# A three-block network on one core: part of VectorE's elementwise work moved to GpSimd, a residual factor folded into a weight, and new instruction orders

## The chip, the cores and the metric

The kernel runs on one core of a Trainium2 chip. The time is the device time of one execution in microseconds, for the whole program: loading of the weights, their preparation, and 16 samples. The kernel before was run three times: 1011.65, 1012.00 and 1012.29 us, median 1012.0.

## The reference, cut to what matters

Input `x` has 16 samples of 256 tokens and 128 channels. Each goes through two blocks with layer norms around them; the first is a state-space mixer with an MLP, then attention with an MLP, the second a gated feed-forward network of width 512. The lines that matter here:

```python
h = layernorm(x)                                  # x0 of the first block
xm = resid_mix_m[0] * h + resid_mix_m[1] * h      # first mix
Bm, Cm = xm @ B_proj_w, xm @ C_proj_w             # 16 heads of 64
value, gate = split(rms_norm(xm) @ in_proj_w)     # 256 + 256
value = silu(causal_conv(value))
y = selective_scan(value, A, Bm, Cm, dt) + D_param * value
y = (y * silu(gate)) @ out_proj_w                 # gate product
xm = xm + mamba_scale * y
xm = xm + m_mlp_scale * (relu(rms_norm(xm) @ m_fc_w) ** 2 @ m_proj_w)
xa = resid_mix_a[0] * xm + resid_mix_a[1] * h     # second mix
...                                               # attention, o_proj, MLP: xa
x1 = x + layernorm(xa)
f = silu(n @ w1) * (n @ w2)                       # n = layernorm(x1)
f = gelu(gelu(f @ h1) @ h2) @ w3
out = x1 + layernorm(f)                           # last addition
```

## The kernel before, in words

A sample of 256 tokens is two tiles of 128 tokens. Elementwise work on tokens has the shape 128x256 (two tiles of 128 channels); the transposed work has channels on the partitions and 256 tokens along the row. Products that need more precision are split in a high and a low part: ScalarE writes the rounded high part, VectorE or GpSimd subtract it for the low part, and TensorE makes three products (hi x hi, lo x hi, hi x lo). That is `xmT_hi`/`xmT_lo` after xm_turn, `nT`, `n2T`, `xT`, and `hD_hi`/`hD_lo` of the feed-forward block, whose low part GpSimd makes in four subtractions a sample (two in hd_part at L612 ahead of hidden1, two in hc_part at L617 ahead of hidden2).

All 16 samples run through nine chains of steps, named by letters: N (load, norm), M (projections, convolution), S (the scan), D (output projection, MLP, second mix), H (head of attention), K (row maxima), A (weights and values), T (tail of attention, its MLP), F (feed-forward). W is the preparation of the weights, run once. A step is a small function on each engine that takes part in it. Every engine has an order written out by hand, a string of letters in `TURNS`: for each letter the engine takes the next step of that chain, whichever sample it is at. So an engine works on up to seven samples at a time, and in the regular part of the program it goes from the scan of sample i to the feed-forward block of sample i-6. An engine never overtakes its own order; between engines there are semaphores. `BANKS` says, in the same way, which of the eight PSUM banks each step of TensorE takes; its former holder must have been read out. `FILL` says before which TensorE steps how many filling products, of the identity with itself and of no use to the result, are made.

Names that matter here: `xh` the normalised input, `xm` the mixer's stream, `val`/`yg` one buffer for value and gated value, `gate` the gate, `xa` the stream of the attention block, `rows` the channel factors (R_M0, R_A0, R_A1), `LM` the decay matrices of the scan, `P` the exponentials (P01, P2), `sl` the evacuated attention output, `bank` any PSUM bank. The steps on the way of the change:

- norm_in, norm_in2 (VectorE, GpSimd, ScalarE): statistics, layer norm into `xh` (L953), first mix into `xm` (L978), squares and norm of `xm`.
- mask (VectorE, L1011): scan products times `LM`; va (TensorE) multiplies by the values; yg (VectorE, L1016 and L1019) adds D and multiplies by the gate; m_out (TensorE) projects.
- m_norm (VectorE, L1032): `xh` times R_A1. m_res (VectorE, L1039, L1041, L1043): adds the MLP's sum, multiplies by R_A0, adds `xh` into `xa`.
- wts (TensorE, QT,KT), wt (ScalarE, L827, exponential), pmask (GpSimd, L549), pv (TensorE, P,Va), y_rows (TensorE, from `sl`).
- f_norm (VectorE, L953 and L1216): last layer norm and last addition.
- GpSimd also makes every reciprocal root, as a pair of tiny instructions (L501, L503), the two squares in each MLP (L527, L560) and, at the start, the preparation of weights (L581 to L607).

Of the kernel before, what the change touches and what calls it, by code (L numbers as in the profile page):

```python
# [48 lines left out]
    ssq_f=TILES, rs_f_eps=1, rs_f=1, nrm_f=1, n2_hi=1, hid_f=2, mlp_f=1, mlp_free=1, mix=2, xa=1,  # L49
# [38 lines left out]
def _chains():  # L88
# [4 lines left out]
    front = [("load_x", 0), ("norm_in", 0), ("norm_in2", 0), ("nrm_in", 0)]  # L93
    mixer = [("xm_turn", 0), ("n_turn", 0)] + several("gates", 2) + several("conv", 2) + [("val", 0), ("val_turn", 0)]
    mixed = several("m_out", 2) + [("m_add", 0), ("m_sq", 0), ("m_norm", 0), ("n2_turn", 0)]
# [3 lines left out]
    for u in range(KINDS):  # L99
# [112 lines left out]
def program(nc, t, out):  # L212
# [167 lines left out]
    def wait_free(engine, c, i, n):  # L380
# [101 lines left out]
    def _(pool):  # L482
# [100 lines left out]
        def by_row(w, r, nk):  # L583
            g.tensor_tensor(w[:], w[:], r.unsqueeze(1).to_broadcast([P, nk, D]), ALU.mult)
# [1042 lines left out]
```

## Time and profile before

| | |
|---|---|
| runs | 1011.65, 1012.00, 1012.29 us |
| profiled execution | 1011.6 us, of which the span from first to last instruction is 1009.9 |
| granted TensorE clock, mean | 0.994 |
| TensorE busy | 934.5 us, 93% |
| VectorE busy | 707.6 us, 70% |
| ScalarE busy | 649.3 us, 64% |
| GpSimd busy | 388.1 us, 38% |
| bytes moved | 14.49 MB, mean 14 GB/s |

The busy share of TensorE counts its filling products as well. The first 250 us bring the samples one after another into the pipeline, the last 180 us drain it. The rows on which the prediction rests have a section of their own below.

### The profile page before, as it was taken

What the parts mean: (1) busy time and instruction counts of PE and PEld (TensorE: products, weight loads), DVE (VectorE), ACT (ScalarE), POOL (GpSimd) and SP (SyncE); (2) the same over time, 40 slices, a digit from 0 to 9 for tenths busy, and PEclk for the clock granted to TensorE, in tenths of its full rate; (3) what the DMA queues carried; (4) which work ended last, traced back from release to release, by engine and by line L of the source; (5) the groups of instructions that cost most, each with busy time, mean ns of one, the idle gap of its engine ahead of it and who ended that gap; (6) DMA issues with size and microseconds to landing.
All of it is one profiled execution on the core that took longest, in us unless ns stands there. A gap on an engine that the chain in (4) does not pass through costs nothing.

```text
span 1009.9 us, 25012 instructions
## 1 busy us (share of the span) xinstructions
PE 934.5 (93%) x9570; PEld 805.3 (80%) x9570; DVE 707.6 (70%) x2075; ACT 649.3 (64%) x1513; POOL 388.1 (38%) x625
## 2 busy tenths in 40 slices
PE   6889999998999989999999999899999999999996
PEld 6778788766978878697878878697878877878896
DVE  4556898977878676968868686968868686853330
ACT  3654546858658577775757677775757678578541
POOL 2553112325143333525244343525244336355421
PEclk9999999999999999999999999999999999999999
DMA  7000000000000000000000000000000000000000
GB/s 272 1 1 7 7 6 2 13 2 12 2 17 2 1 18 1 18 1 17 2 17 2 6 14 1 18 2 17 2 17 2 7 6 7 12 7 7 16 6 6
DMA packets 17206, 14.49 MB, mean 14 GB/s; under 512 B 1857, under 2 KB 15553, under 8 KB 16833
## 3 DMA queue, kind: packets, MB, share of 16 engines
q1 hardware_dynamic: 17088, 12.89, 4.0%
q8 instruction: 78, 1.28, 0.5%
q14 instruction: 40, 0.32, 0.1%
HBM read 10.79 MB, written 2.10 MB: 13 GB/s over the span
## 4 chain that ended last, share of the span: by engine, by line
PE 61%; ACT 17%; DVE 8%; POOL 7%; issue 5%; DMA 0%; SPq 0%; POOLq 0%; ACTq 0%; DVEq 0%
PE bank L1233 57%; POOL hD_lo L617 4%; ACT P L827 3%; POOL hD_lo L612 2%; ACT h L860 2%; PE bank L1244 2%; ACT junk L668 2%; ACT L860 1%; DVE cv L998 1%; DVE mneg L1140 1%; DVE M L1011 1%; ACT sl L835 1%; ACT BC L675 1%; ACT LM L662 1%; POOL P L549 1%
## 5 line engine op out<-in xcount | busy, mean ns | idle before, releaser
L549 POOL TENSOR_SCALAR_AFFINE_SELECT P<-P 128x256 f32<-128x256 f32 (+1 forms) x192 | 94.2, 506 | 181.2 <-ACT P L827 175.9
L1011 DVE TENSOR_TENSOR M<-bank,LM 128x384 f32<-128x384 f32 x256 | 126.7, 550 | 50.7 <-PE bank L1233 50.5
L1233 PE MATMUL bank<-hD_hi,w_h_hi 128*128 128x256 f32 x512 | 147.7, 289 | 12.6 <-POOL hD_lo L617 9.5
L1233 PE MATMUL bank<-hD_hi,w_h_lo 128*128 128x256 f32 x512 | 143.4, 280 | 0.0
L1233 PE MATMUL bank<-hD_lo,w_h_hi 128*128 128x256 f32 x512 | 143.4, 280 | 0.0
L1140 DVE TENSOR_REDUCE mneg<-bank 128x2 f32<-128x512 f32 (+1 forms) x192 | 121.6, 682 | 12.1 <-PE bank L1233 12.0
L827 ACT ACTIVATE P<-bank 128x512 f32<-128x512 f32 x192 | 101.2, 612 | 17.6 <-PE bank L1233 16.8
L1233 PEld LDWEIGHTS bank<-hD_hi,w_h_hi 128*128 128x128 f32 x512 | 96.4, 188 | 17.7 <-POOL hD_lo L617 12.8
L866 ACT ACTIVATE h<-bank,cols 128x256 f32<-128x256 f32 x128 | 53.2, 471 | 87.6 <-PE bank L1233 87.1
L675 ACT ACTIVATE BC<-bank 128x512 f32<-128x512 f32 x128 | 75.1, 606 | 51.2 <-PE bank L1233 48.8
L1233 PE MATMUL bank<-BC 64*128 64x256 f32 (+1 forms) x1024 | 101.0, 336 | 4.7 <-ACT BC L675 2.9
L1233 PEld LDWEIGHTS bank<-BC 64*128 64x128 f32 x1024 | 84.2, 187 | 20.1 <-ACT BC L675 5.6
L1233 PEld LDWEIGHTS bank<-hD_lo,w_h_hi 128*128 128x128 f32 x512 | 96.5, 188 | 0.0
L1233 PEld LDWEIGHTS bank<-hD_hi,w_h_lo 128*128 128x128 f32 x512 | 96.3, 188 | 0.0
L617 POOL TENSOR_TENSOR hD_lo<-h,hD_hi 128x512 fp32r<-128x512 f32 x32 | 42.7, 1355 | 105.6 <-ACT hD_hi L876 105.6
L1233 PE MATMUL bank<-ident 128*128 128x128 f32 x514 | 71.7, 285 | 12.1 <-DMA M<-in_w_in 7.5
L1233 PEld LDWEIGHTS bank<-ident 128*128 128x128 f32 x514 | 64.8, 198 | 16.0 <-issue 8.6
L942 DVE BATCH_NORM_STATS2 ostat<-bank 128x6 f32<-128x128 f32 x32 | 7.9, 290 | 89.9 <-PE bank L1233 89.9
L998 DVE SCALAR_TENSOR_TENSOR cv<-vpad,cols,cv 128x256 f32<-128x256 f32 x96 | 53.2, 555 | 3.4
L1233 PE MATMUL bank<-M,xpad 128*32 128x256 f32 (+1 forms) x1024 | 54.1, 332 | 1.0 <-DVE M L1011 0.9
L527 POOL TENSOR_TENSOR hid<-hid 128x512 f32<-128x512 f32 x32 | 33.4, 1050 | 53.4 <-ACT hid L773 53.1
L612 POOL TENSOR_TENSOR hD_lo<-h,hD_hi 128x512 fp32r<-128x512 f32 x32 | 40.7, 1283 | 32.1 <-ACT hD_hi L715 31.5
(252 smaller groups left out, 2599.0 us busy)
## 6 DMA issues: line engine op xcount, KB each, us to landing
xh<-in_x SPq DMA_DIRECT2D x16, 128.0 KB, 2.1
P<-in_w_h SPq DMA_DIRECT2D x2, 1024.0 KB, 8.2
x_res<-in_x SPq DMA_DIRECT2D x16, 128.0 KB, 2.3
out<-out_sb SPq DMA_DIRECT2D x16, 128.0 KB, 2.2
M<-in_w_B SPq DMA_DIRECT2D x1, 512.0 KB, 4.3
M<-in_w_C SPq DMA_DIRECT2D x1, 512.0 KB, 4.8
Qs<-in_w SPq DMA_DIRECT2D x2, 256.0 KB, 4.3
M<-in_w_in SPq DMA_DIRECT2D x1, 256.0 KB, 3.2
```

Source lines behind the costliest of these rows:

```text
L527: g.tensor_tensor(two, two, two, ALU.mult).then_inc(S["hid_f"], 1)
L549: g.affine_select(p3, p3, [[0, parts], [1, P]], ALU.is_ge, zero, base=0, channel_multiplier=-1).then_inc(S["pmask"], 1)
L612: g.tensor_tensor(hD_lo[:, two, :], h[:, two, :], hD_hi[:, two, :].bitcast(F32), ALU.subtract).then_inc(S["hd_lo"], 1)
L617: g.tensor_tensor(hD_lo[:, two, :], h[:, two, :], hD_hi[:, two, :].bitcast(F32), ALU.subtract).then_inc(S["hc_lo"], 1)
L675: a.activation(dst, psum(c, i, n) if src is None else src, ACT.Copy).then_inc(evac(c, n), 1)
L827: a.activation(PT[c][:, j, :], psum("A", i, n), ACT.Exp).then_inc(evac("A", n), 1)
L860: a.activation(h[:, j, :], psum_t("F", i, F_W + j), ACT.Silu, scale=cols[:, C_W1 + j:C_W1 + j + 1]).then_inc(S["silu"], 1)
L866: last = a.activation(h[:, j, :], psum("F", i, n)[:, k * TOK:(k + 1) * TOK], ACT.Gelu, scale=cols[:, c + j:c + j + 1])
L998: v.scalar_tensor_tensor(cv[:, b, :], vpad[:, b, j:j + L], w(j), cv[:, b, :], ALU.mult, ALU.add).then_inc(S["conv"], 1)
L1011: last = v.tensor_tensor(M[:, k % 2, r, e, :], psum("C", i, 2 * n + e)[:, 0:TRI], LM[:, h + e, :, :].rearrange("p a q -> p (a q)"), ALU.mult)
L1140: v.reduce_max(neg, of, axis=AX.X, negate=True).then_inc(evac("K", n), 1)
L1233: return p.matmul(o, lhsT, rhs, start=start, stop=True, skip_group_check=True)
```

## The change

Five edits go together.

1. The residual factor R_A0 = resid_mix_a[0] is multiplied into the weight `w_mpj` of the mixer's MLP, once at the start, on GpSimd. The sum that `down` leaves in PSUM then already has the factor.
2. The second mix gets a step m_mix on GpSimd, of three instructions: `xh` times R_A1, `xm` times R_A0, and their sum into `xh`. On VectorE m_norm's product is gone, and of m_res one addition is left, `xh` plus PSUM into `xa`.
3. The gate product (yg) goes from VectorE to GpSimd. VectorE keeps the addition of D ahead of it.
4. The first mix (mix_in) and, with it, the sum of the two factors at sample 0, goes to GpSimd.
5. The last addition (f_norm) goes to GpSimd; VectorE keeps the layer norm ahead of it.

`TURNS`, `BANKS` and `FILL` are new for all engines. There are 257 filling products before and 241 after. The diff, cut to its core:

```diff
-    ssq_f=TILES, rs_f_eps=1, rs_f=1, nrm_f=1, n2_hi=1, hid_f=2, mlp_f=1, mlp_free=1, mix=2, xa=1,
+    ssq_f=TILES, rs_f_eps=1, rs_f=1, nrm_f=1, n2_hi=1, hid_f=2, mlp_f=1, by_a1=1, by_a0=1, mix=1, xa=1,
...
-    front = [("load_x", 0), ("norm_in", 0), ("norm_in2", 0), ("nrm_in", 0)]
+    front = [("load_x", 0), ("norm_in", 0), ("mix_in", 0), ("norm_in2", 0), ("nrm_in", 0)]
...
-    PE=("MMMMMMSSSSSMSMMSSSSSSSDSSSSDSSSSMSSSSSSSSDSDDSSDDDDHDHMDDMDDSMSMSSSSMSSHSSSSHSDSMSKSKMSSSSMDKMSDDDMSSDSDSSSKSSHSDMSSMKSM"
+    PE=("MMMMMMSSSSSSMMSSSSSSSSDSSSSMDSSSMSSSSSSSSDSDDSSDDDDHHDDDMMDSSMMSSSDSMSSHSSSSSMHSKMKSSSSSMDDSSMKDDMDSSDSDSSSSSKSMHSSMKSMS"
...
# GpSimd
+        def mix_in(i, _):
+            if i == 0:
+                pool.wait_ge(first_in, 16 * len(first_w))
+                g.tensor_tensor(rows[:, R_M0, :], rows[:, R_M0, :], nrm[:, 0, :], ALU.add).then_inc(row_in, 1)
+                pool.wait_ge(row_in, 1)
+            if i > 1:
+                pool.wait_ge(S["xa"], i - 1)
+            pool.wait_ge(S["nrm_n"], 2 * i + 1)
+            g.tensor_tensor(xm[i % 2][:], xh[i % XBUF][:], by_channel(R_M0), ALU.mult).then_inc(S["xm"], 1)
+
+        def yg_(i, b):
+            pool.wait_ge(S["yacc_free"], at(i, "yacc_free", b + 1))
+            g.tensor_tensor(yg[:, b, :], yg[:, b, :], gate[:, b, :], ALU.mult).then_inc(S["yg"], 1)
+
+        def m_mix(i, _):
+            x, r = xh[i % XBUF], xm[i % 2]
+            pool.wait_ge(S["xm"], i + 1)
+            g.tensor_tensor(x[:], x[:], by_channel(R_A1), ALU.mult).then_inc(S["by_a1"], 1)
+            pool.wait_ge(S["nrm_f"], i + 1)
+            g.tensor_tensor(r[:], r[:], by_channel(R_A0), ALU.mult).then_inc(S["by_a0"], 1)
+            pool.wait_ge(S["by_a0"], i + 1)
+            g.tensor_tensor(x[:], x[:], r[:], ALU.add).then_inc(S["mix"], 1)
+
+        def f_norm(i, _):
+            pool.wait_ge(S["nrm_o"], i + 1)
+            g.tensor_tensor(out_sb[:], out_sb[:], x1[i % 2][:], ALU.add).then_inc(S["out_ready"], 1)
...
         def w_mix(i, _):
             pool.wait_ge(mixer_in, 16 * len(mixer_w))
             by_row(w_out, rows_m[:, R_MS, :], 2)
-            by_row(w_mpj, rows_m[:, R_MM, :], NBLK)
+            by_row(w_mpj, rows_m[:, R_MM, :], NBLK).then_inc(mpj_scaled, 1)
+            pool.wait_ge(mpj_scaled, 1)
             pool.wait_ge(mix_half, 1)
+            by_row(w_mpj, rows[:, R_A0, :], NBLK)
...
# VectorE
         def norm_in2(i, _):
             x = xh[i % XBUF]
-            if i > 1:
-                dve.wait_ge(S["xa"], i - 1)
             dve.wait_ge(S["rs_n"], 2 * i + 1)
             layer_norm(x, x, nmv, nrs).then_inc(S["nrm_n"], 1)
...
-            dve.wait_ge(S["nrm_n"], 2 * i + 1)
-            v.tensor_tensor(xm[i % 2][:], x[:], by_channel(R_M0), ALU.mult).then_inc(S["xm"], 1)
...
-            dve.wait_ge(S["yacc_free"], at(i, "yacc_free", b + 1))
-            v.tensor_tensor(yg[:, b, :], yg[:, b, :], gate[:, b, :], ALU.mult).then_inc(S["yg"], 1)
...
-        def m_norm(i, _):
-            x = xh[i % XBUF]
-            dve.wait_ge(S["xm"], i + 1)
-            v.tensor_tensor(x[:], x[:], by_channel(R_A1), ALU.mult).then_inc(S["mix"], 1)
...
         def m_res(i, _):
...
+            dve.wait_ge(S["mix"], i + 1)
             dve.wait_ge(S["mlp_f"], i + 1)
-            v.tensor_tensor(flat(x), flat(x), psum_t("Y", i, 1), ALU.add).then_inc(S["mlp_free"], 1)
-            dve.wait_ge(S["mlp_free"], i + 1)
-            v.tensor_tensor(x[:], x[:], by_channel(R_A0), ALU.mult).then_inc(S["mix"], 1)
-            dve.wait_ge(S["mix"], 2 * i + 2)
-            v.tensor_tensor(xa[i % ABUF][:], x[:], xh[i % XBUF][:], ALU.add).then_inc(S["xa"], 1)
+            v.tensor_tensor(flat(xa[i % ABUF]), flat(xh[i % XBUF]), psum_t("Y", i, 1), ALU.add).then_inc(S["xa"], 1)
...
         def f_norm(i, _):
...
-            dve.wait_ge(S["nrm_o"], i + 1)
-            v.tensor_tensor(out_sb[:], out_sb[:], x1[i % 2][:], ALU.add).then_inc(S["out_ready"], 1)
```

The new tables rearrange every engine. Three places show how.

TensorE in the regular part, from the last `wts` of sample 6 (QT,KT) to its `pv` (P,Va). `ident,sl` are the transposes of y_rows, `w_out,val` m_out of sample 9, `ident,bn` x2_turn of sample 4, `Kb,Qb` and `later,picks` scores of sample 7. Before:

```order
L1233 MATMUL bank<-QT,KT 128x512 x4
L1486 MATMUL bank<-ident,sl 128x128 x4
L1233 MATMUL bank<-w_out,val 128x128 x4
L1244 MATMUL bank<-ident,bn 128x128 x2
L1233 MATMUL bank<-Kb,Qb 128x256 x8
L1233 MATMUL bank<-later,picks 128x2x32 x16
L1233 MATMUL bank<-P,Va 32x512 x4
```

Now, where `w_o,ya` is o_proj of sample 5:

```order
L1239 MATMUL bank<-QT,KT 128x512 x4
L1239 MATMUL bank<-w_o,ya 128x128 x2
L1492 MATMUL bank<-ident,sl 128x128 x4
L1239 MATMUL bank<-w_out,val 128x128 x2
L1250 MATMUL bank<-ident,bn 128x128 x2
L1239 MATMUL bank<-w_out,val 128x128 x2
L1239 MATMUL bank<-Kb,Qb 128x256 x8
L1239 MATMUL bank<-later,picks 128x2x32 x16
L1239 MATMUL bank<-P,Va 32x512 x4
```

The output projection of an earlier sample comes ahead of the transposes of `sl`, and the two halves of m_out are apart.

TensorE at the program's start, where `ident` alone is a filling product. Before:

```order
L1233 MATMUL bank<-ident 128x128 x22
L1244 MATMUL bank<-ident,xm 128x128 x2
L1233 MATMUL bank<-ident 128x128 x8
L1244 MATMUL bank<-ident,nrm_n 128x128 x2
L1233 MATMUL bank<-ident 128x128 x3
```

The same place on TensorE now:

```order
L1239 MATMUL bank<-ident 128x128 x27
L1250 MATMUL bank<-ident,xm 128x128 x2
L1239 MATMUL bank<-ident 128x128 x11
L1250 MATMUL bank<-ident,nrm_n 128x128 x2
L1239 MATMUL bank<-ident 128x128 x3
```

The first transposes, of `xm`, have 27 filling products ahead of them where they had 22, and those of `nrm_n` 11 where they had 8.

GpSimd at the start, from the roots of sample 1 on. `nms`/`nrs` are a reciprocal root's pair, `LM` the selects of the decay matrices, the `w` rows the preparation of weights. Before:

```order
L501 TENSOR_TENSOR nms<-nmv,eps_ln 128x2
L503 TENSOR_TENSOR nrs<-nms,half 128x2
L581 AFFINE_SELECT LM<-LM 128x4x256 x4
L501 TENSOR_TENSOR nms<-ss_n,eps_rms 128x2
L503 TENSOR_TENSOR nrs<-nms,half 128x2
L584 TENSOR_TENSOR w_out<-w_out,hid 128x256
L584 TENSOR_TENSOR w_mpj<-w_mpj,hid 128x512
L591 TENSOR_TENSOR w_mfc_lo<-hid,w_mfc_hi 128x512
```

GpSimd from the same roots on now:

```order
L499 TENSOR_TENSOR nms<-nmv,eps_ln 128x2
L501 TENSOR_TENSOR nrs<-nms,half 128x2
L522 TENSOR_TENSOR xm<-xh,rows 128x256
L499 TENSOR_TENSOR nms<-ss_n,eps_rms 128x2
L501 TENSOR_TENSOR nrs<-nms,half 128x2
L609 AFFINE_SELECT LM<-LM 128x4x256 x4
L612 TENSOR_TENSOR w_out<-w_out,hid 128x256
L612 TENSOR_TENSOR w_mpj<-w_mpj,hid 128x512
L612 TENSOR_TENSOR w_mpj<-w_mpj,rows 128x512
L621 TENSOR_TENSOR w_mfc_lo<-hid,w_mfc_hi 128x512
L526 TENSOR_TENSOR val<-val,gate 128x256
```

The second pair of sample 1, from the squares `ss_n`, now stands ahead of the selects on `LM`, the first mix of sample 1 with it, and the gate product of sample 0 (`val<-val,gate`) comes ahead of a group of weights.

## Rows read from the trace of the kernel before

**Rows 1.** the page, busy time of the engines

```profile
PE 934.5 (93%) x9570; PEld 805.3 (80%) x9570; DVE 707.6 (70%) x2075; ACT 649.3 (64%) x1513; POOL 388.1 (38%) x625
```

**Rows 2.** busy time in a stretch, seven samples; columns: span, then each engine

```profile
380.18:778.71 398.53, 379.01 (x3981) 324.57 (x3979) 303.27 (x897) 275.51 (x652) 159.17 (x260) 1.00 0.03 9
```

**Rows 3.** TensorE's waits, 380.18 to 778.71; columns: total us, times, longest

```profile
PE bank L1233 <- POOL hD_lo L617: 4.3, 7, 0.8
PE bank L1233 <- POOL P L549: 3.9, 8, 0.5
PE bank L1233 <- DVE xmT_lo L983: 3.3, 7, 0.9
PE bank L1486 <- ACT sl L835: 1.8, 5, 0.4
...
PE bank L1233 <- ACT sl L835: 0.8, 1, 0.8
```

**Rows 4.** VectorE by line; columns: busy us, mean ns, idle before

```profile
L1019 DVE TENSOR_TENSOR val<-val,gate 128x256 f32<-128x256 f32 x32 | 14.9, 467 | 1.1
...
L1216 DVE TENSOR_TENSOR out_sb<-out_sb,x 128x256 f32<-128x256 f32 x16 | 8.1, 504 | 0.6
...
L1032 DVE TENSOR_TENSOR xh<-xh,rows 128x256 f32<-128x256 f32 x16 | 7.8, 489 | 0.0
...
L1043 DVE TENSOR_TENSOR xa<-xm,xh 128x256 f32<-128x256 f32 x16 | 7.1, 446 | 0.5
L978 DVE TENSOR_TENSOR xm<-xh,rows 128x256 f32<-128x256 f32 x16 | 6.8, 426 | 0.5
L1041 DVE TENSOR_TENSOR xm<-xm,rows 128x256 f32<-128x256 f32 x16 | 6.8, 425 | 0.6
```

**Rows 5.** GpSimd by line, two products of the weights

```profile
L584 POOL TENSOR_TENSOR w_out<-w_out,hid 128x256 f32<-128x256 f32 x1 | 0.7, 729 | 0.0
...
L597 POOL TENSOR_TENSOR w_o<-w_o,bhid 128x128 f32<-128x128 f32 x1 | 0.5, 462 | 0.0
```

**Rows 6.** GpSimd by line, the subtraction ahead of hidden2

```profile
L617 POOL TENSOR_TENSOR hD_lo<-h,hD_hi 128x512 fp32r<-128x512 f32 x32 | 42.7, 1355 | 105.6 <-ACT hD_hi L876 105.6
```

**Rows 7.** TensorE in order of time, 469 to 473 us

```profile
470.15 0.66 PE L1486 MATMUL bank<-ident,sl 128*128 128x128 f32 x4 [0.34 <-ACT sl L835]
...
472.91 0.64 PE L1233 MATMUL bank<-P,Va 128*32 128x512 f32 x4 [0.54 <-POOL P L549]
```

**Rows 8.** TensorE in order of time, first 17 us

```profile
7.51 6.86 PE L1233 MATMUL bank<-ident 128*128 128x128 f32 x44 [7.51 <-DMA M<-in_w_in]
...
14.43 1.95 PE L1233 MATMUL bank<-ident 128*128 128x128 f32 x16
16.21 0.38 PE L1244 MATMUL bank<-ident,nrm_n 128*128 128x128 f32 x2
```

**Rows 9.** all engines in order of time, 29 to 40 us

```profile
29.25 1.10 POOL L581 TENSOR_SCALAR_AFFINE_SELECT LM<-LM 128x1024 f32<-128x1024 f32 x1 [0.34 <-ACT LM L662]
...
35.15 0.61 ACT L645 ACTIVATE w_mfc_hi<-hid 128x512 fp32r<-128x512 f32 x1
...
38.03 0.32 ACT L668 ACTIVATE junk<-xm 128x128 bf16<-128x128 f32 x1
...
39.09 0.69 POOL L503 TENSOR_TENSOR nrs<-nms,half 128x2 f32<-128x2 f32 x1
39.27 1.02 DVE L1011 TENSOR_TENSOR M<-bank,LM 128x384 f32<-128x384 f32 x2 [7.88 <-PE bank L1233]
```

**Rows 10.** GpSimd and VectorE in order of time, 45 to 50 us

```profile
45.80 1.33 POOL L599 TENSOR_TENSOR w_afc_lo<-bhid,w_afc_hi 128x512 fp32r<-128x512 f32 x1
...
46.03 2.43 DVE L998 SCALAR_TENSOR_TENSOR cv<-vpad,cols,cv 128x256 f32<-128x256 f32 x3
...
48.82 1.53 DVE L998 SCALAR_TENSOR_TENSOR cv<-vpad,cols,cv 128x256 f32<-128x256 f32 x3
```

**Rows 11.** the page, the convolution steps of VectorE

```profile
L998 DVE SCALAR_TENSOR_TENSOR cv<-vpad,cols,cv 128x256 f32<-128x256 f32 x96 | 53.2, 555 | 3.4
```

More of the change, by code:

```diff
@@ L92, in _chains @@
     weights_in = [("w_heads", 0), ("w_first", 0), ("w_scale", 0)] + several("w_split", 2) + several("w_decay", BATCHES) + [("w_mix", 0), ("w_back", 0), ("w_ffn", 0)]
[L93 removed]
+    front = [("load_x", 0), ("norm_in", 0), ("mix_in", 0), ("norm_in2", 0), ("nrm_in", 0)]
     mixer = [("xm_turn", 0), ("n_turn", 0)] + several("gates", 2) + several("conv", 2) + [("val", 0), ("val_turn", 0)]
[L95 removed]
+    mixed = several("m_out", 2) + [("m_add", 0), ("m_sq", 0), ("m_norm", 0), ("n2_turn", 0), ("m_mix", 0)]
     mixed += several("up", 2) + several("down", 2) + [("m_res", 0)]
@@ new lines @@
+FILL = {("bc", 0, 0): 1, ("gates", 0, 0): 3, ("n3_turn", 0, 0): 9, ("n_turn", 0, 0): 11, ("qkv", 0, 0): 2,
+        ("sc", 0, 0): 16, ("sc", 0, 1): 2, ("sc", 0, 3): 2, ("val_turn", 0, 0): 16, ("xm_turn", 0, 0): 27,
+        ("gate", 1, 0): 2, ("gates", 1, 0): 3, ("o_proj", 1, 0): 1, ("sc", 1, 3): 1, ("scores", 1, 2): 4,
+        ("up", 1, 0): 5, ("wts", 1, 0): 2, ("wts", 1, 1): 3, ("xm_turn", 1, 0): 8, ("n2_turn", 2, 0): 1,
+        ("n_turn", 2, 0): 6, ("sc", 2, 1): 2, ("scores", 2, 0): 6, ("up", 2, 0): 4, ("wts", 2, 0): 2,
+        ("y_rows", 2, 0): 1, ("pv", 3, 1): 1, ("sc", 3, 0): 2, ("sc", 3, 3): 2, ("scores", 3, 0): 1,
+        ("n2_turn", 4, 0): 2, ("n3_turn", 4, 0): 2, ("sc", 4, 1): 3, ("sc", 5, 1): 3, ("n2_turn", 7, 0): 1,
+        ("scores", 7, 2): 1, ("pv", 9, 1): 1, ("scores", 9, 2): 2, ("x2_turn", 9, 0): 3, ("scores", 10, 2): 1,
+        ("x2_turn", 12, 0): 5, ("q2_turn", 13, 0): 2, ("bc", 14, 0): 2, ("gate", 14, 0): 6, ("hidden2", 14, 0): 6,
+        ("n4_turn", 14, 0): 2, ("o_proj", 14, 0): 2, ("gate", 15, 0): 11, ("hidden1", 15, 0): 12, ("hidden2", 15, 0): 13,
+        ("o_proj", 15, 0): 2, ("scores", 15, 0): 2, ("up_b", 15, 0): 6, ("wts", 15, 1): 5}
@@ L617, in hc_part @@
             g.tensor_tensor(hD_lo[:, two, :], h[:, two, :], hD_hi[:, two, :].bitcast(F32), ALU.subtract).then_inc(S["hc_lo"], 1)
-        pipeline("Pool", dict(norm_in=norm_in, norm_in2=norm_in2, m_sq=m_sq, up=up, a_sq=a_sq, v_in=v_in, pmask=pmask, o_sq=o_sq, up_b=up_b,
+        pipeline("Pool", dict(norm_in=norm_in, mix_in=mix_in, norm_in2=norm_in2, yg=yg_, m_mix=m_mix, f_norm=f_norm, m_sq=m_sq, up=up, a_sq=a_sq, v_in=v_in, pmask=pmask, o_sq=o_sq, up_b=up_b,
                               res_b=res_b, ln_a2=ln_a2, f_stats=f_stats, w_decay=w_decay, w_mix=w_mix, w_back=w_back, w_ffn=w_ffn, hd_part=hd_part, hc_part=hc_part))
```

113 lines of the change are left out of this document (49 added, 64 removed), and 3 rows, old and new, of the table FILL.

## The prediction, made before the changed kernel was run

> **What bounds the kernel now.** I read the page first: TensorE is busy 93% of the span, VectorE 70%, ScalarE 64%, GpSimd 38% [rows 1]. That busy share contains the filling matmuls on the identity, so the next view is a stretch in the regular part. From one pair of `hD_lo` subtractions (380.18 us) to the one seven samples later (778.71) there are 398.53 us, 56.9 us a sample. TensorE is busy 379.01 of them and VectorE 303.27 [rows 2]. A sample thus costs 54.1 us of TensorE and 2.8 us in which it stands still; no relief of another engine can give more than those 2.8 us a sample there.
>
> Then I asked for whom TensorE waits in that stretch. It is a handful of short waits that come back in every sample: GpSimd's `hD_lo` before `hidden2` 4.3 us in 7 times, GpSimd's masks on `P` before `pv` 3.9 us, VectorE's `xmT_lo` before `bc` 3.3 us, ScalarE's copy `sl` before `y_rows` 1.8 us and 0.8 us in a second row [rows 3]. Per sample: 0.61, 0.56, 0.47 and 0.37 us. These five rows make 14.1 us, 2.0 a sample; the rest of the 19.5 us that TensorE stands still is in smaller ones. Of the five only the third is VectorE's own. The engine that the change relieves is seldom the one TensorE waits for, so what it can bring comes through the new order of TensorE's work.
>
> **What leaves VectorE.** Each of the 16 samples loses seven VectorE instructions: two gate products, the first mix, the product by R_A1, the product by R_A0, one of three additions in m_res, and the last addition: 14.9 + 6.8 + 7.8 + 6.8 + 7.1 + 8.1 = 51.5 us, 3.2 a sample [rows 4]. (m_res keeps one addition, as long as L1039's.) By itself that is worth near nothing, VectorE having 95 us of idle time in the 398.5.
>
> **What comes to GpSimd.** Also seven instructions of 128x256 a sample, 112 in all: mix_in, two yg, three in m_mix, f_norm. The trace has one two-input product of this size on GpSimd, `w_out`, at 729 ns, and one of half the size at 462 [rows 5]. The sum takes 0.73 us: 82 us, 5.1 a sample, which brings GpSimd from 388 to 470 us, 47% of the span. Bounds for the size: 0.46 below, and above it 1.36 us, the `hD_lo` of twice the size [rows 6], or 52 to 152 us. Where do they stand? m_mix (2.2 us) and mix_in lie after m_sq, ahead of the `hD_lo` that `hidden2` needs; there GpSimd was idle 105.6 us in 16 samples, 6.6 each [rows 6], so the cover is three times the need. The gate product is the one on a path: val to yg to m_out. It grows from 0.47 to 0.73 us and gains a hop between engines; in the order some 5 us of TensorE's work stand between `va` and m_out's second half, before and now alike, so I cost it at nothing; with the cover gone it would cost 0.3 to 0.5 us a sample. The folding of R_A0 into w_mpj is one more product of 128x512 during the start, about 1.3 us of GpSimd, needed only at `down` of sample 0, more than 20 us later: nothing.
>
> **What the new order of TensorE does.** Here the gain should be. Between the last `wts` (QT,KT) of sample 6 and its `pv` (P,Va), TensorE waited 0.34 us for `sl` at 470.15 and 0.54 us for the mask at 472.91 [rows 7]. Now o_proj (the `w_o` matmuls, some 0.5 us) is drawn in ahead of the transposes of `sl`. Over samples 3 to 12 I counted in the order: in all ten, o_proj, one of m_out's halves or `down`'s second half now stands ahead of those transposes (before in three); in nine there is more work than before between that `wts` and `pv`. I take 0.33 of the 0.37 us and 0.35 of the 0.56. Between `hidden1` and `hidden2` four of the seven regular samples (3 to 9) get the first `sc`, k_turn or both, 0.3 to 1.6 us more cover against a wait of 0.61: I take 0.3. `xm_turn` and `bc` get a `gate` between them in three of ten samples: 0.1 of the 0.47. Together 1.08 us a sample. Against it stand new short waits that a rearranged order always opens somewhere, and the hop to GpSimd ahead of xm_turn; I set 0.2 by choice. Net 0.9 us a sample, over the 700 us from 120 to 820, 12.3 samples of 56.9 us: **-11.1 us**. Bounds for this term: all 2.8 us a sample (-34), or none of it.
>
> **The start.** It gets later. Before, xm_turn of sample 0 was held by 22 filling matmuls (44 passes in 6.86 us), then 8 more took 1.95 us, and the transposes of `nrm_n` began at 16.21 [rows 8]. Now there are 27 and 11. Eight fills at 1.79/8 = 0.22 us (14.43 to 16.21) would be +1.8 us; moreover ScalarE now takes the squares of sample 0 only after `xmT_hi`. From the start of such squares to the end of GpSimd's pair behind them the trace has 1.75 us (38.03 to 39.78) [rows 9]. So: the five fills more put xm_turn's end near 15.7, `xmT_hi` 0.4, squares and pair 1.75, the norm 0.6, and the transposes start at 18.4 or so: +2.1. VectorE's w_heads ahead of the first layer norm, and the first mix on GpSimd, hide under the fills. Next, the first product with `LM`. Before, it started at 39.27, when `LM` had long been masked on GpSimd, the first select from 29.25 [rows 9]. Now GpSimd does norm_in2 of sample 1 first, and that waits for ScalarE's squares, at 38.03 before. ScalarE has two copies of 128x512 fewer ahead of them (w_mfc_hi at 35.15 and one of the same form, some 0.5 us each of its queue): 38.03 - 1.0 + 2.1 = 39.1, squares and pair 1.75, one select 1.1: 42.0 against 39.27, **+2.7 us**. I carry it through, since TensorE in the regular part is too full to make it good. Bounds: 0 (conv and the deferred weight work absorb it) and 5.
>
> **The end.** The last samples' chain through hidden1 and hidden2 has the same order on all engines. The last addition goes from 0.50 to 0.73 us plus a hop: **+0.3 us**.
>
> **Contention between VectorE and GpSimd.** While GpSimd subtracts w_afc_lo (45.80 to 47.13), three conv steps of VectorE take 2.43 us; the next three, with GpSimd waiting, take 1.53 [rows 10]. So 1.33 us of GpSimd held VectorE up for 0.9. The 5.1 us a sample that GpSimd gains could in the worst case cost VectorE 5.1 x 0.9/1.33 = 3.5 us, all that was taken from it (3.2). In the regular part such meetings are rarer: the conv steps average 555 ns over the whole run [rows 11] against 1.53/3 = 510. I take nothing for it in the sum, VectorE having 24% to spare, and keep it for the slow side.
> The Trainium skill ("SBUF — State Buffer", section "SBUF: two separate sides") says of this that GpSimd and a VectorE instruction with two SBUF inputs share a port pair that one of them holds for the whole instruction while the other stands. By that rule, the trace agrees: the stretched steps have two SBUF inputs. It speaks against the change, since the seven instructions leave VectorE and still can lock it; its time is that of the third case below.
>
> **Sum.** -11.1 + 2.7 + 0.3 = -8.1 us on the profiled execution's 1011.6 (span 1009.9): 1003.5. The median of the runs is 1012.0, 0.4 higher, so **1003.9 us**.
>
> **The cases.**
> 1. The forecast, 994 to 1010, at 1003.9: chance 0.53.
> 2. Nearly all waits go, because the order found cover for each: 2.2 us x 12.3 = -27, +3.0: 988. For: no wait of the five rows is longer than 0.9 us. Against: 10.8 of their 14.1 us are ended by GpSimd or ScalarE, whose work does not shrink. Chance 0.06.
> 3. Slower: GpSimd's queue and the lock. A product on GpSimd ends later by 0.26 us, by a hop of 0.1 and by half a VectorE instruction that holds it, 0.25: 0.6 us later in yg and in mix_in, 0.3 more for what queues behind them (`P`'s masks after yg). If that reaches TensorE, +0.9 x 12.3 = +11, +3.0: 1026; it decides once the work between `va` and m_out, or between the last `wts` and `pv`, is shorter than the lengthened chain. For: `P`'s masks are already waited for. Against: GpSimd's idle 6.6 us a sample, 47% load. Chance 0.25 for all that ends above 1014.
> 4. No change that can be told: the covers win 0.2 to 0.3 us a sample, and the start takes it back: 1012. For: the stretch from wts to hidden1 is filled by ScalarE, which keeps its work, and a gap closed in TensorE may open a few instructions later. Chance 0.16.
>
> A measurement of this kernel can tell 0.2%, 2 us, from no change. Faster: 0.53 + 0.06 = 0.59; same 0.16; slower 0.25. The range holds 8 in 10 from 994 to 1018: about 0.1 is left below it and 0.1 above.
>
> **What would show it.** In the profile after: VectorE near 660 us busy (707.6 - 51.5 and a little stretch), GpSimd near 470. TensorE's idle time per regular sample down from 2.8 to about 1.9, those for `sl` gone, those for `P` and for the second `hD_lo` half as long. The first LM product near 42 us. Wrong would be: a new wait of TensorE for `val` or `xm` on GpSimd, stretched conv steps (well above 555 ns in the mean), or TensorE waits that move to `n_turn`, `gates` or `sc` with the period still 56.9 us.

## The result, and the profile after

The changed kernel takes 1004.95 us (1003.70 to 1005.41, 4 runs) against 1011.83; the ratio is 0.993, with a 95% interval of 0.9913 to 0.9947. 1003.9 was forecast. The gain is 0.7%, clear of the scatter but small. The rows below show that the sum came out near for reasons that are only in part those given.

The page's busy line, then the regular stretch between the same two `hD_lo` pairs as in [rows 2], seven samples; columns: span, busy time of TensorE, of its weight loads, of VectorE, ScalarE and GpSimd (with the count of instructions), mean granted clock, then two on transfers.

```profile
PE 931.7 (93%) x9538; PEld 803.6 (80%) x9538; DVE 673.9 (67%) x1962; ACT 646.3 (64%) x1511; POOL 465.4 (46%) x739
```

```profile
379.01:774.74 395.73, 379.06 (x3983) 326.35 (x3982) 291.55 (x849) 275.63 (x653) 190.33 (x309) 1.00 0.03 8
```

TensorE's busy time in the stretch is the same to 0.05 us. What shrank is the time it stands still, from 19.5 to 16.7 us, and with it the period from 56.9 to 56.5 us. Its waits in this stretch (total us, times, longest), the answer to [rows 3]:

```profile
PE bank L1250 <- ACT nrm L715: 3.0, 5, 1.1
PE bank L1239 <- DVE h L1211: 2.0, 6, 0.7
PE bank L1239 <- POOL hD_lo L647: 1.8, 4, 0.6
PE bank L1239 <- DVE xmT_lo L1002: 1.7, 4, 1.0
PE bank L1239 <- POOL P L577: 1.5, 4, 0.8
PE bank L1411 <- DVE Kb L1122: 1.2, 1, 1.2
PE bank L1239 <- DVE x L1195: 1.0, 4, 0.3
```

The four causes of [rows 3] made 14.1 us and make 5.0; `sl` is gone. But `nrm` (3.0 us), `Kb` (1.2) and `x` (1.0) were not in the list of before at all, and the rows for VectorE's `h` grew from 1.5 to 2.5 us. Of the smaller rows of before, `bn` on ScalarE (1.7 us) is gone.

The moved work on GpSimd by line (busy us, mean ns, idle before), and two groups that answer to [rows 6] and [rows 11]:

```profile
L526 POOL TENSOR_TENSOR val<-val,gate 128x256 f32<-128x256 f32 x32 | 23.3, 730 | 31.0 <-DVE val L1035 30.9
L522 POOL TENSOR_TENSOR xm<-xh,rows 128x256 f32<-128x256 f32 x16 | 13.8, 861 | 17.2 <-DVE xh L983 17.2
...
L533 POOL TENSOR_TENSOR xm<-xm,rows 128x256 f32<-128x256 f32 x16 | 11.8, 736 | 1.4 <-ACT nrm L715 1.3
```

```profile
L647 POOL TENSOR_TENSOR hD_lo<-h,hD_hi 128x512 fp32r<-128x512 f32 x32 | 41.0, 1300 | 100.0 <-ACT hD_hi L906 100.0
```

```profile
L1017 DVE SCALAR_TENSOR_TENSOR cv<-vpad,cols,cv 128x256 f32<-128x256 f32 x96 | 56.3, 586 | 3.4
```

A product of 128x256 takes 730 ns. The first mix has a mean of 861 because one of its 16, that of sample 1, took 2.77 us; the others took 0.72 to 0.74. It ran beside two subtractions on VectorE, and all the inputs lie in SBUF:

```profile
30.14 2.77 POOL L522 TENSOR_TENSOR xm<-xh,rows 128x256 f32<-128x256 f32 x1 [0.72 <-DVE xh L983]
```

```profile
29.98 1.22 DVE L959 TENSOR_TENSOR w_B_lo<-M,w_B_hi 128x1024 fp32r<-128x1024 f32 x1
31.11 1.22 DVE L959 TENSOR_TENSOR w_C_lo<-M,w_C_hi 128x1024 fp32r<-128x1024 f32 x1
```

Ahead of the `hD_lo` of `hidden2` GpSimd still has 100.0 us of idle time, 5.6 us less than before. The conv steps grew by 31 ns each.

One of the recorded signs of being wrong, a wait of TensorE for `xm` on GpSimd, did show, once, at the start, at 33.0 us:

```profile
PE bank L1250 <- POOL xm L522: 3.2, 1, 3.2
```

It has an equal in the kernel before, 2.2 us for the same `xm` from VectorE with 19 filling products ahead of it where there are 8 now. With the first mix back on VectorE (e6 below) it is 3.0 us, so GpSimd is not what makes it long.

The start, in order of time: the second run of fills that leads to the transposes of `nrm_n` (16.21 in [rows 8]), the selects of `LM`, and the first LM product (39.27 in the prediction):

```profile
19.55 0.44 PE L1250 MATMUL bank<-ident,nrm_n 128*128 128x128 f32 x2 [0.70 <-ACT nrm_n L715]
```

```profile
42.08 2.15 POOL L609 TENSOR_SCALAR_AFFINE_SELECT LM<-LM 128x1024 f32<-128x1024 f32 x2
```

```profile
43.22 1.02 DVE L1030 TENSOR_TENSOR M<-bank,LM 128x384 f32<-128x384 f32 x2 [2.74 <-POOL LM L609]
```

The transposes are 3.3 us later than before and the first product 3.95 us. Yet the second `hD_lo` pair of sample 0 starts at 264.11 instead of 263.44: 0.7 us is left. That pair, of sample 0 and of sample 15, is the ruler for all kernels here. "Still" is the width of the interval less TensorE's busy time in it; times are medians, ratios against the kernel before. The last three columns are of one profiled execution each, and that is not always a typical one: those of e3, e7 and e9 are the fastest of their kernels, 3.6, 2.2 and 5.3 us below the median.

| kernel | time, us | ratio, interval | pair 0 | pair 0 to 15 | still |
|---|---|---|---|---|---|
| before | 1011.8 | | 263.4 | 729.5 | 39.8 |
| after | 1005.0 | 0.993 (0.9913 to 0.9947) | 264.1 | 722.3 | 34.0 |
| e1 orders only | 1010.3 | 0.9995 (0.9982 to 1.0008) | 262.8 | 730.4 | 38.9 |
| e9 orders, m_mix replaced | 1007.9 | 0.997 (0.9952 to 0.9987) | 261.5 | 723.2 | 35.3 |
| e2 move only | 1035.5 | 1.0231 (1.0218 to 1.0244) | 279.1 | 738.1 | 45.3 |
| e10 move in part | 1024.6 | 1.0128 (1.0113 to 1.0143) | 275.2 | 732.1 | 42.9 |
| e3 yg back | 1006.0 | 0.9941 (0.9921 to 0.996) | 262.8 | 721.5 | 33.7 |
| e5 m_mix back | 1006.8 | 0.996 (0.9946 to 0.9975) | 263.0 | 724.9 | 37.5 |
| e6 mix_in back | 1005.0 | 0.993 (0.9916 to 0.9944) | 264.8 | 722.6 | 34.3 |
| e4 GpSimd +32 | 1012.9 | 1.0005 (0.9993 to 1.0018) | 265.6 | 729.1 | 39.8 |
| e11 cover for sl | 1012.6 | 1.0013 (1.0002 to 1.0023) | 263.2 | 730.0 | 40.1 |
| e7 start, 8 fills less | 1004.2 | 0.9923 (0.9909 to 0.9937) | 262.2 | 721.6 | 34.5 |
| e8 15 fills more | 1004.5 | 0.9931 (0.992 to 0.9943) | 263.3 | 722.9 | 34.1 |
| e12 three together | 1003.8 | 0.9929 (0.9917 to 0.9941) | 264.1 | 721.4 | 33.7 |

### The profile page after: what moved, and what is told of

Its sections match the earlier page's. It is cut to its first block, busy times and chain, and to the rows that moved or that the text cites. A ratio compares the mean times of both kernels' runs of the same rounds, so it can differ in the third digit from the quotient of the medians.

```text
span 1003.0 us, 24950 instructions
## 1 busy us (share of the span) xinstructions
PE 931.7 (93%) x9538; PEld 803.6 (80%) x9538; DVE 673.9 (67%) x1962; ACT 646.3 (64%) x1511; POOL 465.4 (46%) x739
## 4 chain that ended last, share of the span: by engine, by line
PE 61%; ACT 14%; POOL 9%; DVE 8%; issue 6%; DMA 0%; SPq 0%; ACTq 0%; POOLq 0%; DVEq 0%
PE bank L1239 57%; POOL hD_lo L647 3%; POOL P L577 2%; PE bank L1250 2%; ACT h L890 2%; POOL hD_lo L642 2%; ACT P L857 2%; DVE M L1030 2%; ACT h L896 1%; ACT junk L698 1%; DVE cv L1017 1%; ACT L890 1%; ACT sl L865 1%; ACT BC L705 1%; ACT LM L692 1%
## 5 line engine op out<-in xcount | busy, mean ns | idle before, releaser
L577 POOL TENSOR_SCALAR_AFFINE_SELECT P<-P 128x256 f32<-128x256 f32 (+1 forms) x192 | 92.0, 495 | 74.3 <-ACT P L857 71.2
L1239 PE MATMUL bank<-ident 128*128 128x128 f32 x482 | 67.0, 287 | 8.0 <-DMA M<-in_w_in 7.1
L1239 PEld LDWEIGHTS bank<-ident 128*128 128x128 f32 x482 | 61.4, 201 | 10.1 <-issue 8.0
L1017 DVE SCALAR_TENSOR_TENSOR cv<-vpad,cols,cv 128x256 f32<-128x256 f32 x96 | 56.3, 586 | 3.4
L499 POOL TENSOR_TENSOR oms<-omv,eps_ln 128x2 f32<-128x2 f32 x16 | 3.4, 213 | 106.6 <-DVE omv L977 106.4
L1239 PE MATMUL bank<-P,Va 128*32 128x256 f32 (+1 forms) x512 | 47.9, 491 | 5.3 <-POOL P L577 4.8
```

What stands on the lines that cost most here:

```text
L577: g.affine_select(p3, p3, [[0, parts], [1, P]], ALU.is_ge, zero, base=0, channel_multiplier=-1).then_inc(S["pmask"], 1)
L1017: v.scalar_tensor_tensor(cv[:, b, :], vpad[:, b, j:j + L], w(j), cv[:, b, :], ALU.mult, ALU.add).then_inc(S["conv"], 1)
L1239: return p.matmul(o, lhsT, rhs, start=start, stop=True, skip_group_check=True)
```

## Experiments: the orders without the move

**e1.** The changed kernel's orders of TensorE, ScalarE and SyncE, banks and fills, all seven instructions on VectorE (R_A0 stays folded into the weight):

```diff
-        pipeline("Pool", dict(norm_in=norm_in, mix_in=mix_in, norm_in2=norm_in2, yg=yg_, m_mix=m_mix, f_norm=f_norm, ...
+        pipeline("Pool", dict(norm_in=norm_in, norm_in2=norm_in2, ...
+        pipeline("DVE", dict(m_mix=m_mix, mix_back=mix_back, ...
```

> The new orders of TensorE, ScalarE and SyncE and the new banks and fills as they are in the changed kernel, but the seven moved instructions a sample are back on VectorE: gate product and last addition right behind the instruction that feeds them, first mix and the three of the second mix at the points at which GpSimd did them. Theory (the gain is the order of TensorE's work, the relief of VectorE is worth near nothing): 1003 to 1007 us, ratio to the kernel before 0.991 to 0.995, VectorE busy near 700 us, GpSimd near 385. Rival (the relief itself is needed: the new order is tight for VectorE): the gain is lost, 1010 us or more, with new TensorE waits ended by VectorE of 0.3 us a sample or more.

1010.3 us, no gain left. The rival's figure. TensorE's waits in the regular stretch, 379 to 779 us:

```profile
PE bank L1437 <- DVE Kb L1146: 3.2, 1, 3.2
...
PE bank L1265 <- DVE M L1052: 1.7, 4, 1.0
```

Both are ended by VectorE, and both were shorter in the changed kernel (1.2 and 0.5). In this execution the 3.2 us cost more than themselves. Busy time and granted clock around that wait, 4 us a row:

```profile
509.00:513.00 4.00, 0.77 (x20) 0.53 (x10) 3.97 (x7) 0.00 (x0) 4.00 (x5) 1.00 0.00 0
513.00:517.00 4.00, 4.00 (x24) 4.00 (x23) 2.09 (x5) 2.28 (x4) 0.35 (x1) 0.57 0.00 0
```

TensorE was busy 0.77 of 4 us, and in the next 4 us the clock stood at its lower level, 1.2 GHz, for most of the row: mean 0.57, a loss of 0.43 x 4 = 1.7 us. Between the pairs e1 takes 8.1 us more than the changed kernel. Of these TensorE stands still for 4.9; the other 3.2 are busy time (691.5 against 688.4 us for the same 7036 matmuls), which goes with three stretches at the lower clock in e1 (at 513, 537 and 708 us) and one in the changed kernel (at 535). The conv steps of VectorE are as short again as in [rows 11]:

```profile
L1039 DVE SCALAR_TENSOR_TENSOR cv<-vpad,cols,cv 128x256 f32<-128x256 f32 x96 | 53.0, 552 | 3.4
```

**e5** puts m_mix alone back on VectorE.

> The changed kernel with the three products and sums of the second mix (m_mix) alone back on VectorE, at the point at which GpSimd did them. With all seven instructions back the time was 1010.3, with the gate product alone back 1006.0, as in the changed kernel. Theory now (the new order is tight for VectorE, and m_mix, three instructions in a row, is the largest piece taken from it): 1008 to 1011 us, with the waits for Kb and h grown as they did with all seven back. Rival (the first mix is the piece that counts): 1004 to 1006 us.

1006.8 us, between the two figures; its interval only just touches the changed kernel's. In its profile "still" grew by 3.5 us, at samples 4, 8 and 9. One such place, VectorE's order at 742 us:

```profile
742.63 0.39 DVE L1006 TENSOR_TENSOR xh<-xh,rows 128x256 f32<-128x256 f32 x1
742.94 0.42 DVE L1008 TENSOR_TENSOR xm<-xm,rows 128x256 f32<-128x256 f32 x1
743.39 0.42 DVE L1010 TENSOR_TENSOR xh<-xh,xm 128x256 f32<-128x256 f32 x1
743.73 1.94 DVE L1043 TENSOR_TENSOR M<-bank,LM 128x384 f32<-128x384 f32 x4
```

and what TensorE did there:

```profile
745.00 0.50 PE L1252 MATMUL bank<-QT,KT 26*128 26x512 f32 x4 [1.04 <-DVE M L1043]
```

Three small instructions, 1.1 us together, stand ahead of the masks, and TensorE waits 1.04 us for the masks. VectorE had just been idle for 2.36 us, from 739.13 to 741.49. So the loss could be one of place.

**e9** takes e1 and moves m_mix, from sample 4 on, to where VectorE was idle 1.9 us or more:

```diff
# in words, one of twelve places (times of e5 and of e9)
-    VectorE's order: m_mix(13) behind the statistics of `xa` at 742.6 us, ahead of four masks
+    VectorE's order: m_mix(13) ahead of the next conv, at 709.0 us
```

> All seven instructions a sample back on VectorE in the new orders, as in the first experiment, with one difference: from sample 4 on the three of the second mix stand where VectorE waited for TensorE for 1.9 us or more in the changed kernel, and not at the point at which GpSimd did them. With the latter the time was 1010.3 us. Theory A (VectorE's room is enough; what the first experiment lost was my placing of m_mix ahead of masks that TensorE waits for): 1004 to 1007 us. Theory B (the new orders need the relief of VectorE itself): 1009 us or more.

1007.9 us, ratio 0.997: neither theory. In its profile the interval between the pairs is 723.2 us, 0.9 above the changed kernel's, so most of e1's loss in schedule was my place for m_mix. The wait for `Kb` is still there, 3.2 us at 510 us, but this time the clock stayed full behind it. That execution is the fastest of eight (1002.6 us, mean granted clock 0.993); the two with the lowest clock took 1012.3 us (0.984) and 1010.8 us (0.985), where the changed kernel's runs had 0.991 to 0.994. At the median over half of the gain is missing: the orders without the move keep 0.3% of the 0.7. That the clock takes a good part of the rest is inferred from these figures only, and one run with 0.993 took 1009.0 us; why it is granted less there stays open.

**e3 and e6** put single pieces back, the gate product and the first mix.

```diff
             v.scalar_tensor_tensor(yg[:, b, :], ... ALU.mult, ALU.add).then_inc(S["yacc_free"], 1)
+            dve.wait_ge(S["yacc_free"], at(i, "yacc_free", b + 1))
+            v.tensor_tensor(yg[:, b, :], yg[:, b, :], gate[:, b, :], ALU.mult).then_inc(S["yg"], 1)
```

> The changed kernel with the gate product alone back on VectorE, right behind the addition of D, which frees GpSimd of 32 products (23 us). Theory (the gate product costs nothing on GpSimd, its path to m_out has cover): 1004 to 1006 us, no difference to the changed kernel above 0.2%. Rival (0.6 us later in yg is on the path, in part of the samples): 2 to 6 us faster than the changed kernel, 999 to 1003 us.

> The changed kernel with the first mix (mix_in) alone back on VectorE, one instruction a sample. Theory (m_mix is the piece that counts, or the sum of all): 1004 to 1006.5 us. Rival (mix_in counts: it stands in VectorE's queue ahead of the masks and rope steps of other samples, or it is waited for itself): 1008 us or more. In the old orders its place on GpSimd cost 2.0 to 2.6 us in four samples, so a third way is open too: 1002 us or less, if GpSimd is the worse place in the new order as well.

Neither differs from the changed kernel by more than the intervals, so neither group, 32 and 16 of the 112 moved instructions, is needed for the gain by itself. The two together, the last addition alone, and the folded factor alone were not tried; nor were the new banks and fills apart from the new orders.

## Experiments: the move without the orders

**e2.** The orders, banks and fills of before, and each moved instruction in GpSimd's order at the point at which VectorE did it.

```diff
# in words
-TURNS, BANKS, FILL of after
+TURNS, BANKS, FILL of before; GpSimd's row with mix_in, yg, m_mix, f_norm put in by time
```

> The orders, banks and fills of the kernel before, with the seven instructions a sample on GpSimd, each put into GpSimd's order at the point at which VectorE did it, and R_A0 folded into the weight. Theory: worth near nothing or a little slower, 1011 to 1016 us: the TensorE waits ended by GpSimd (P and hD_lo, 9.2 us of the regular stretch before) grow where a product of 0.73 us stands ahead of them. Rival (the move itself carries the gain): 1006 us or less.

1035.5 us: far outside both. Of the 23.7 us, 15.7 are lost before the first pair, and 11.3 of these in one wait for the gate product of sample 0:

```profile
PE bank L1242 <- POOL val L529: 11.4, 2, 11.3
```

On GpSimd that product stood behind w_ffn, the preparation of the last weights, with two subtractions of 8.9 us together. The rest is lost later, mainly here (TensorE's waits, 397 to 804 us; then GpSimd and TensorE at 612 us):

```profile
PE bank L1253 <- POOL xm L525: 8.7, 6, 2.6
PE bank L1242 <- POOL P L580: 4.5, 11, 0.9
```

```profile
609.78 0.77 POOL L534 TENSOR_TENSOR xh<-xh,rows 128x256 f32<-128x256 f32 x1
610.52 0.72 POOL L536 TENSOR_TENSOR xm<-xm,rows 128x256 f32<-128x256 f32 x1
611.32 0.73 POOL L538 TENSOR_TENSOR xh<-xh,xm 128x256 f32<-128x256 f32 x1
612.00 0.72 POOL L525 TENSOR_TENSOR xm<-xh,rows 128x256 f32<-128x256 f32 x1
```

```profile
612.78 0.44 PE L1253 MATMUL bank<-ident,xm 128*128 128x128 f32 x2 [2.03 <-POOL xm L525]
```

m_mix of one sample, 2.2 us in a row, stands ahead of mix_in of another, and xm_turn waits 2.03 us for it. Both are my third case, slower through GpSimd's queue, and the recorded "new wait of TensorE for `val` or `xm` on GpSimd". With the new orders neither is left in the regular part.

**e10** leaves mix_in on VectorE and puts w_ffn behind the first two samples' work.

```diff
# in words, against e2
-        # mix_in in GpSimd's order; w_ffn ahead of yg(0,1)
+        # mix_in back in norm_in2 on VectorE; w_ffn behind v_in(0), at 94 us
```

> The orders, banks and fills of the kernel before with the gate product, the second mix and the last addition on GpSimd, but the first mix left on VectorE, and GpSimd's preparation of the last weights (w_ffn, 13 us) put behind them at 92 us, where it had 9.7 us of idle time. With the first mix moved as well, and w_ffn ahead of the gate product of sample 0, it was 1035.5: 15.7 us lost before 280 us, 14.7 us waited for xm. Theory (those two places are the whole loss, and the rest of the move is worth nothing in the old orders): 1010 to 1014 us. Rival (a move into old orders costs wherever it is made): 1018 us or more.

1024.6 us, the rival's side. Between the pairs it is 732.1, 2.7 us above before, so without the first mix the move costs little in the regular part. The rest is lost at the start, and most of it in one place. VectorE beside GpSimd's w_ffn:

```profile
96.31 4.46 DVE L1107 SCALAR_TENSOR_TENSOR qs<-qs 128x40 f32<-128x40 f32 x1
100.80 4.42 DVE L1105 TENSOR_TENSOR qs<-qs 128x40 f32<-128x40 f32 x1
105.25 0.20 DVE L1106 SCALAR_TENSOR_TENSOR qs<-qs 128x40 f32<-128x40 f32 x1
```

```profile
96.18 8.98 POOL L637 TENSOR_TENSOR w_h_lo<-P,w_h_hi 128x2048 fp32r<-128x2048 f32 x2
```

An instruction of 0.20 us takes 4.46, as long as one of GpSimd's two. VectorE delivered `qn` at 106.4, and TensorE had waited 7.0 us for it. From 102.0 to 112.2 us the granted clock was 0.50; TensorE worked 5.7 us of that, which costs about 2.9 more. The two make 9.9 of the 11.7 us lost before the first pair. Without them the time would be near 1014.7 us, an estimate: just above my theory's range and below the rival's. So the two places were most of the loss, and I had made a third.

## Experiments: GpSimd's slack, the cover, the start

**e4.** One more product of the same size on GpSimd ahead of each gate product (the gate enters squared).

```diff
+            g.tensor_tensor(gate[:, b, :], gate[:, b, :], gate[:, b, :], ALU.mult).then_inc(again, 1)
+            pool.wait_ge(again, 2 * i + b + 1)
             g.tensor_tensor(yg[:, b, :], yg[:, b, :], gate[:, b, :], ALU.mult).then_inc(S["yg"], 1)
```

> The changed kernel with one more 128x256 product on GpSimd ahead of each gate product (the gate is squared, so the output differs): 32 instructions more, 23 us, and the gate product later by 0.73 us and a hop. Theory (the slack of GpSimd and the cover of yg are larger than this): up to +2 us over the changed kernel, 1005 to 1007. Rival (the queue of GpSimd decides, my third case): +0.5 us or more a sample, 1011 us or more, with TensorE waits for P, hD_lo or val grown.

1012.9 us, 7.9 more than the changed kernel for 23 us of GpSimd. The rival held. TensorE's waits, 379 to 784 us; `P` goes from 1.5 to 3.6 us, once 2.2 us long, and `x` from 1.0 to 2.0:

```profile
PE bank L1242 <- POOL P L580: 3.6, 5, 2.2
...
PE bank L1242 <- DVE x L1198: 2.0, 4, 1.0
```

GpSimd at 48% busy has no free slack: 0.25 us of the total for each instruction put ahead of the gate product, while taking the product itself away (e3) gave nothing. The edge lies between the two. These rows don't separate the later gate product from what queues behind it; over the whole run TensorE's waits for `val` on GpSimd grew from 0.2 to 1.2 us and those for `P` from 4.8 to 7.9, so the queue behind it is the larger part.

**e11.** The kernel before, with o_proj moved ahead of the transposes of `sl` in samples 3 to 12.

```diff
-o_proj(i-1) ... down(i+2) pv(i,0) wts(i,2) y_rows(i,0)
+... down(i+2) pv(i,0) wts(i,2) o_proj(i-1) y_rows(i,0)
```

> The kernel before with one step of TensorE moved in samples 3 to 12: o_proj of the sample ahead, from its place ahead of down to just ahead of y_rows, so that it stands between the last wts and the transposes of sl. My recorded step (cover for sl is worth 0.33 us a sample): 3.3 us less, ratio 0.9967. Rival (the wait only moves: what o_proj leaves behind opens there, or the gap comes back at the next wait): 0 to 1 us less, the waits for sl gone and others grown.

Ratio 1.0013, no gain. In the regular stretch the 1.8 us row for `sl` is gone (the second, of 0.8, stays) and `P` on GpSimd fell from 3.9 to 2.5, but this row grew:

```profile
PE bank L1233 <- ACT P L827: 2.2, 8, 0.4
```

The exponentials on ScalarE, for which TensorE waited 0.3 us before. The gap moved, as the rival said.

**e7** takes 8 fills out of sample 0, **e8** puts 15 in.

```diff
-("n_turn", 0, 0): 11, ("xm_turn", 0, 0): 27
+("n_turn", 0, 0): 8, ("xm_turn", 0, 0): 22
```

```diff
-("n3_turn", 0, 0): 9, ("xm_turn", 1, 0): 8
+("n3_turn", 0, 0): 13, ("xm_turn", 1, 0): 19
```

> The changed kernel with the fills of sample 0 as before at two steps: 22 instead of 27 ahead of xm_turn, 8 instead of 11 ahead of n_turn. They are 1.8 us at 0.22 us a fill. My recorded step (the start is carried through to the end one for one): 1.8 us less, 1003.0 to 1003.5. Rival, from the trace after (4 us late at the first LM product, 0.7 us late at 264 us: the time is made good on the way): within 0.6 us of the changed kernel.

> The changed kernel with 15 more fills between 20 and 264 us, as many as the kernel before had more there: 19 instead of 8 ahead of xm_turn of sample 1, 13 instead of 9 ahead of n3_turn of sample 0. Theory (the fills left out are what made the late start good): 2 to 3.4 us over the changed kernel, 1007 to 1008.5. Rival (they stand in time in which TensorE waits anyway): 1004 to 1005.5.

e7 is 0.8 us below the changed kernel. The intervals, for the difference some 2 us either way, tell this neither from nothing nor from the 1.8 of my step. Its profile, of the fastest run, reaches the first pair 1.9 us earlier than the changed kernel's: 1.1 us are there at the transposes of `xm` of sample 1, and the lower clock behind 60 us lasts half as long.

e8, 15 more fills, is not slower; my theory for the start falls, and the rival holds. Eleven of the fifteen stand in the wait for `xm` at 33 us that is shown above: it goes from 3.2 to 0.8 us, by the 2.4 us that eleven fills of 0.22 take. The clock differs as well; 60 to 68 us, first the changed kernel, then e8:

```profile
60.00:68.00 8.00, 6.40 (x40) 5.44 (x42) 2.03 (x5) 2.33 (x4) 4.26 (x4) 0.57 0.00 0
```

```profile
60.00:68.00 8.00, 7.08 (x70) 6.27 (x70) 3.29 (x7) 4.41 (x7) 5.60 (x4) 1.00 0.00 0
```

In both a wait of 3.2 us for the masks of sample 0 lies ahead of these matmuls (it ends at 61.6 and 60.9 us). Behind it the clock is at 0.57 in the changed kernel, up to 0.43 x 8 = 3.4 us lost, and full in e8. But that isn't shown to be the work of the fills: e5, which has the changed kernel's fills, has the same wait and the full clock there too.

**e12** joins e3, e7 and the larger part of e8 (11 fills).

> The changed kernel with three edits that each cost nothing alone: the gate product back on VectorE, sample 0's fills at 22 and 8, and 19 instead of 8 fills ahead of xm_turn of sample 1. If they add up: 1002 to 1003.5 us. If each only moved time about: 1004 to 1005, as the changed kernel.

1003.8 us, ratio 0.9929: the changed kernel's time within the interval. That the three add up (1002 to 1003.5 us) isn't shown. No version here beats the changed kernel measurably.

## Why the prediction came near

The profiled span went from 1009.9 to 1003.0, -6.9 us against -8.1 forecast. The terms were further off than their sum: the steady one came out 4.0 us smaller, the start 2.0 us and the end 0.8 us better than recorded. That the last two took back 2.8 of the 4.0 is luck. By the recorded steps:

- **Steady term, -11.1: right in kind, mis-sized.** Between the pairs it is -7.1 (729.5 to 722.3), of which 5.8 us is TensorE standing still less. In the regular stretch it is 0.4 us a sample, not 0.9. The recorded covers came out as priced or better: `sl` 2.6 to 0 us (2.3 forecast), `P` 3.9 to 1.5 (2.4), the `hD_lo` 4.3 to 1.8 (2.1), `xmT_lo` 3.3 to 1.7 (0.7), together 9.1 us against 7.6. What failed is the other side, "I set 0.2 by choice" for new waits. All other listed rows went from 4.4 to 10.1 us in seven samples, 0.8 a sample. e11 shows the same on one cover alone: with the wait for `sl` taken away, the time did not fall.
- **"By itself that is worth near nothing", of VectorE's relief: not settled.** The move alone lost 23.7 us (e2), so it gains nothing without new orders. The new orders without the move lost the gain in e1, and m_mix alone on VectorE lost a part (e5). But with m_mix in VectorE's idle times (e9) they kept 0.3 of the 0.7% at the median and nearly the whole schedule in one profile. So a part of the gain needs only the orders, and how much the relief adds once each piece has a good place stays open. Neither the gate product nor the first mix had to move (e3, e6).
- **Start, +2.7: too low at its end point, and not what arrived.** The first LM product is 3.95 us late; of the 1.25 us missed, 1.15 are there at the transposes of `nrm_n` (19.55 against the recorded 18.4). TensorE is 0.7 us late at the first pair. In between something made 3 us good. It isn't the fills left out later (e8). The step "carried through" itself isn't refuted: in e7's profile the 8 fills arrived at the first pair as 1.9 us. The new order may have won time between 43 and 264 us that my sum didn't hold; no run tests this.
- **End, +0.3: right.** From the end of the last layer norm to the issue of the output 0.49 us before and 0.83 after; the last transfer was 0.8 us shorter and hid it.
- **Contention, nothing taken.** VectorE's busy time fell by 33.7 us, not 51.5, and ended at 673.9 instead of near 660. Added up one by one, its instructions fell from 807.7 to 769.8 us, by 37.9, though those taken away made 51.6: the others became 13.7 us longer. Busy time fell by less, since instructions behind one another overlap. The conv steps, named as a sign, are at 586 ns and not 555; with the same orders and the products back on VectorE (e1) they are at 552. So the stretching comes with GpSimd's new work. What it costs in the total was not measured; that the lock can reach TensorE, e10 shows.
- **GpSimd: 465 us, forecast as 470**, 730 ns as taken. Its cover for m_mix and mix_in, 6.6 us against 2.9, was 2.3 times the need and not three. The third case did not come, but e2 and e4 show how it does: m_mix ahead of mix_in, the preparation of weights ahead of a gate product, and one more product ahead of yg. A chance of 0.25 was not too much for it.

## What to carry over

A cover found for one wait is worth what the sum of all waits falls by: here the waits that opened elsewhere took back 5.7 of the 9.1 us covered. Test an order with the loads that it was planned for, and a load in an order that has a place for it: the same seven instructions cost 24 us in the old order and came with a gain in the new one. On an engine without spare time in front of a consumer, the neighbour in the queue matters more than its busy share.

## What the hardware showed

GpSimd's subtraction of 128x2048 held a VectorE instruction with SBUF inputs for its whole length, 4.46 us for 0.20 (e10). In the kernel before, the same subtraction ran twice from 59.5 to 68.8 us, and the masks beside it, one input in PSUM, were not held:

```profile
61.69 1.95 DVE L1011 TENSOR_TENSOR M<-bank,LM 128x384 f32<-128x384 f32 x4 [2.05 <-PE bank L1233]
```

0.49 us each, against 0.55 in the mean of all 256. It goes the other way too: in the changed kernel the first mix of sample 1, begun on GpSimd 0.16 us behind VectorE's first subtraction of 128x1024, took 2.77 us for 0.73 and ended 0.6 us behind the second. The Trainium skill ("SBUF — State Buffer", section "SBUF: two separate sides") says that the shared port pair is locked for a whole instruction, and only against a VectorE instruction with two SBUF inputs or in a two-port mode. By that rule, these traces agree.

Waits of TensorE of 3.0 to 3.25 us stand in the profiles here 15 times behind the first 20 us. With 12 of them the granted clock went to its lower level, 1.2 GHz, within 1.5 us of the wait's end (at 513 us in e1, at 33.4 and 60.8 us in the changed kernel); with three it stayed full (at 61 us in e5 and e8, at 510 us in e9). So such a wait costs its own length and, often but not always, the lower clock behind it, 1.7 us at 513 us and up to 3.4 us at 61 us. And one program was granted mean clocks from 0.984 to 0.996 in its runs (e9), with times from 1002.6 to 1012.3 us, so that one profiled execution may stand 5 us from its median.
